# Two expert tiles in the place of filling transposes, an earlier V evacuation, and convolution taps summed in three accumulators

## The reference

```
x = x + layernorm(attn(layernorm(x)))
x = x + layernorm(ffn(layernorm(x)))

attn(x) = x + h @ Wo,   h = tele + conv + low, with q, k, v = split(x @ Wqkv), 8 heads of 16
  tele: softmax over the keys at distances 0, 1, 2, 4, ..., 512, times v at those distances
  conv: a causal convolution of v, channel by channel, with 7 taps (conv_w)
  low:  linear attention with elu(q)+1 and elu(k)+1, divided by its sum of weights
ffn(x) = sum over 8 experts of gate_e * (gelu(x @ W1[e] + b1[e]) @ W2[e] + b2[e])
         + gelu(x @ Ws1 + bs1) @ Ws2 + bs2
  gate: sigmoid(x @ gate_W) * route_scale, the two largest kept and divided by their sum
```

## Time and profile before

| | |
|---|---|
| median of 3 runs | 281.42 us (281.14 to 282.49) |
| the profiled execution, its own time | 281.83 us |
| its span, first to last instruction | 280.1 us |
| busy share of the span | PE 90%, DVE 82%, ACT 67%, POOL 30% |
| mean granted clock of PE | 0.984 of full speed |
| chain that ended last, by engine | PE 59%, ACT 20%, DVE 10%, POOL 5% |

### The profile page before, as it was taken

One profiled execution on the slowest core, in us unless ns is written; L12 is line 12 of the kernel. 1 busy time (PEld: TensorE's weight loads), 2 busy tenths in 40 slices (PEclk: granted clock), 3 DMA queues, 4 the chain that ended last, 5 costly groups with the idle time before them and its releaser, 6 DMA issues.

```text
span 280.1 us, 4721 instructions
## 1 busy us (share of the span) xinstructions
PE 252.9 (90%) x1630; PEld 176.2 (63%) x1630; DVE 228.3 (82%) x535; ACT 188.8 (67%) x445; POOL 84.5 (30%) x139
## 2 busy tenths in 40 slices
PE   5899999895978899998968899999999799999993
PEld 5444656885435686786625677777655587765483
DVE  7799999879978883999888884989689886975653
ACT  2482256538979676949789867859798356656661
POOL 5960300045471113053371213044242112330023
PEclk9999999997999999999999999999999799999998
DMA  6617801000799963401799963100799954000003
GB/s 197 150 46 241 234 28 50 1 0 9 232 233 194 223 125 67 115 1 50 211 245 194 230 126 68 37 4 20 235 220 238 227 112 83 21 2 1 1 2 112
DMA packets 23394, 32.12 MB, mean 115 GB/s; under 512 B 3957, under 2 KB 17102, under 8 KB 23370
## 3 DMA queue, kind: packets, MB, share of 16 engines
q1 hardware_dynamic: 20346, 21.59, 27.4%
q0 software_dynamic: 3024, 10.22, 19.8%
HBM read 5.07 MB, written 2.10 MB: 26 GB/s over the span
## 4 chain that ended last, share of the span: by engine, by line
PE 59%; ACT 20%; DVE 10%; POOL 5%; issue 3%; DMA 1%; POOLq 0%; DVEq 0%; ACTq 0%
PE psH L1375 11%; PE psF L1437 8%; PE psY L1477 6%; PE psG L1297 4%; PE psA L1269 4%; PE psA L1343 3%; POOL rstd L471 3%; PE psA L1477 3%; DVE prods L286 3%; ACT squares L697 3%; ACT xn L590 2%; PE psG L1463 2%; DVE prods L1026 2%; PE psH L1372 2%; PE psF L1414 2%
## 5 line engine op out<-in xcount | busy, mean ns | idle before, releaser
L286 DVE TENSOR_TENSOR prods<-qT,kT 128x1024 f32<-128x1024 f32 (+1 forms) x48 | 50.6, 1114 | 2.7 <-PE psA L1343 1.6
L469 POOL TENSOR_SCALAR var<-ss 128x4 f32<-128x4 f32 (+1 forms) x24 | 9.8, 408 | 111.9 <-ACT squares L690 49.2
L1375 PE MATMUL psH<-ident,prods 128*128 128x128 f32 x324 | 40.0, 273 | 0.0
L1375 PEld LDWEIGHTS psH<-ident,prods 128*128 128x128 f32 x324 | 36.4, 141 | 2.9 <-issue 2.9
L471 POOL TENSOR_TENSOR rstd<-var,neg_half 128x4 f32<-128x4 f32 (+2 forms) x27 | 34.8, 1288 | 2.3
L1026 DVE TENSOR_TENSOR prods<-v_shift,prob 128x896 f32<-128x896 f32 x32 | 34.5, 1078 | 0.0
L1437 PE MATMUL psF<-x3T,w 128*128 128x512 f32 x58 | 29.1, 612 | 1.8 <-ACT hid L728 1.5
L1148 DVE TENSOR_TENSOR hid<-hid,psG 128x512 f32<-128x512 f32 x30 | 19.4, 682 | 7.6 <-PE psG L1463 7.6
L728 ACT ACTIVATE hid<-psF,b1c 128x512 f32<-128x512 f32 x29 | 19.2, 683 | 7.0 <-PE psF L1437 6.9
L1343 PE MATMUL psA<-prods,slot_sel 128*32 128x512 f32 x168 | 22.6, 597 | 0.9 <-ACT fk_tok L579 0.6
L1026 DVE TENSOR_TENSOR prods<-v_tok,prob 128x128 f32<-128x128 f32 (+2 forms) x60 | 20.6, 373 | 0.6 <-DMA v_shift<-v_tok 0.5
(11 more groups left out here) (241 smaller groups left out, 579.8 us busy)
## 6 DMA issues: line engine op xcount, KB each, us to landing
v_shift<-v_tok SPq DMA_DIRECT2D x20, 448.0 KB
convT<-tapT POOLq DMA_DIRECT2D x6, 512.0 KB, 5.9
x_res<-L_attn_x SPq DMA_DIRECT2D x4, 512.0 KB, 9.8
out<-y_out SPq DMA_DIRECT2D x7, 256.0 KB, 2.3
x_in<-L_attn_x SPq DMA_DIRECT2D x3, 512.0 KB, 4.2
v_shift<-v_tok SPq DMA_DIRECT2D x4, 384.0 KB
tapT<-tapT POOLq DMA_DIRECT2D x3, 512.0 KB, 11.2
convT<-kexp POOLq DMA_DIRECT2D x3, 512.0 KB, 9.1
```

The source lines that it names most:

```text
L286: return eng.tensor_tensor(prods[:, QUADS * (s % 2) + q, t0:t1], qT[:, t0:t1], kT[:, PRE - off + t0:PRE - off + t1], ALU.mult)
L1375: ins = pe.matmul(dst, terms[:, j % TERM_BUFS, m, :], ident[:], is_transpose=True, start=False, stop=(m == live[-1]))
```

## The change

- On PE, in passes 1 to 3, `experts_out(u0, range(0, 2))` stands where the filling transposes ahead of the K projection stood (in pass 3 the second of two fillings). The tiles 2 and 3 take the places that 0 and 1 had, and the block of two tiles behind the turned logits is gone. FILL_K's own wait goes too.
- On ACT, `evacuate_v(b+1)` stands ahead of `normalise3(2b)` instead of behind it (passes 0 to 2), and in passes 1 and 2 `norm2(2b)` stands ahead of `query_parts(b+1)`.
- On POOL, the taps are summed in three accumulators. Before: 0+=1, 2+=3, 0+=4, 2+=5, 0+=6, 0+=2. Now: 0+=1, 2+=3, 4+=5, 0+=2, 4+=6, 0+=4. There are six transfers of the same size in both.
- In the last pass the turning of the gates of the last unit moves ahead of its last hidden chunk on PE and ACT, one expert tile of unit 6 moves behind the spread gates, and DVE takes the small gate steps in other portions between the large products.

```
-N_SUMS, N_SIDE = 4, 2
+N_SUMS, N_SIDE, N_LATE = 3, 1, 2
-LAST_GATE_STEPS = (5, 7, 9, N_GATE_STEPS)
+LAST_GATE_STEPS = (6, 9, N_GATE_STEPS, N_GATE_STEPS)
...
             def sum_taps_second(b):
                 pool.wait_ge(tap_scaled, upto(b - 1, TAPS, 6))
+                add_tap(b, 4, 5, late_added)
+
+            def sum_taps_third(b):
                 pool.wait_ge(sums_added, N_DMA * upto(b - 1, N_SUMS, 1))
+                pool.wait_ge(side_added, N_DMA * upto(b - 1, N_SIDE, 1))
+                add_tap(b, 0, 2, sums_added)
+                pool.wait_ge(tap_scaled, upto(b - 1, TAPS, 7))
+                pool.wait_ge(late_added, N_DMA * upto(b - 1, N_LATE, 1))
+                add_tap(b, 4, 6, late_added)
+                pool.wait_ge(sums_added, N_DMA * upto(b - 1, N_SUMS, 2))
+                pool.wait_ge(late_added, N_DMA * upto(b - 1, N_LATE, 2))
                 add_tap(b, 0, 4, sums_added)
-                pool.wait_ge(side_added, N_DMA * upto(b - 1, N_SIDE, 1))
-                add_tap(b, 2, 5, side_added)
-
-            def sum_taps_third(b):
-                pool.wait_ge(tap_scaled, upto(b - 1, TAPS, 7))
-                pool.wait_ge(sums_added, N_DMA * upto(b - 1, N_SUMS, 2))
-                add_tap(b, 0, 6, sums_added)
-                pool.wait_ge(sums_added, N_DMA * upto(b - 1, N_SUMS, 3))
-                pool.wait_ge(side_added, N_DMA * upto(b - 1, N_SIDE, 2))
-                add_tap(b, 0, 2, sums_added)
...
                         key_parts(b + 1)
+                        if ffn:
+                            norm2(2 * b)
                         query_parts(b + 1)
-                        norm2(2 * b)
+                        if b == 0:
+                            norm2(2 * b)
                         norm3_squares(2 * b)
                         norm2(2 * b + 1)
+                        evacuate_v(b + 1)
                         normalise3(2 * b)
-                        evacuate_v(b + 1)
...
-                    if more and ffn:
-                        pe.wait_ge(hidden_free, upto(u1, N_HIDDEN, -1))
-                        keep_busy(FILL_K, front(u1, X3))
+                    if ffn:
+                        experts_out(u0, range(0, 2))
                     if more:
                         project_k(b + 1)
-                    else:
-                        keep_busy(FILL_LAST, psA[:, 0, :])
                     if ffn:
                         turn_x3(u1)
-                        experts_out(u0, (0,))
+                        experts_out(u0, (2,))
                         gate_logits(u1)
-                        experts_out(u0, (1,))
+                        experts_out(u0, (3,))
                         turn_logits(u1)
-                        experts_out(u0, range(2, TPH))
...
-                    hidden(u1, range(2, 4))
+                    hidden(u1, (2,))
+                    gates_expert_major(u1)
+                    hidden(u1, (3,))
                     experts_out(u0, (0,))
-                    gates_expert_major(u1)
-                    experts_out(u0, (1,))
                     spread_gates(u1, range(0, 4))
-                    experts_out(u0, range(2, TPH))
+                    experts_out(u0, range(1, TPH))
```

More of the change, by code:

```diff
@@ L246, in block_kernel @@
         tap_scaled, sums_added, side_added = sem("tap_scaled"), sem("sums_added"), sem("side_added")
+        late_added = sem("late_added")
         first_ld, first_xn = [sem(f"first_ld{h}") for h in range(2)], [sem(f"first_xn{h}") for h in range(2)]
@@ L856, in _ @@
                     shared_hidden(u0)
-                    hidden(u1, range(0, 3))
+                    hidden(u1, range(0, 1))
                     gates_expert_major(u1)
-                    hidden(u1, range(3, 4))
+                    hidden(u1, range(1, 4))
                     shared_hidden(u1)
```

## The result

| | before | after |
|---|---|---|
| median of 20 runs each | 281.14 us (280.33 to 283.76) | 278.55 us (276.14 to 281.87) |
| the profiled execution, its own time | 281.83 us | 277.38 us |
| its span | 280.1 us | 275.6 us |
| ratio after/before, 95% interval | | 0.9864 [0.9842, 0.9886] |

A forecast was written before the change was run, and what follows sets the result against it. No engine bounds the kernel throughout: PE holds 59% of the chain of waits, ACT 20%. Terms 3.9 + 0.1 + 1.0 + 2.0 = 7.0 us off 281.83 or the 281.42 median gave 274.6 us, own range 274.0 to 275.6, wide range 272.8 to 278.0.

The forecast's parts named there:

- Passes 1 and 2, the tiles: Expert tiles in the filling's place ahead of the K projection: gain of 1.96 us a pass, 3.9 us for two passes.
- norm2 ahead: norm2 before the Q operations on ACT: counted as 0, keeping the tiles' gain; without it up to about 1.5 us a pass lost.
- V early: V evacuated before the third norm on ACT: 1.0 us ahead of pass 3, 0.1 ahead of pass 2, nothing ahead of pass 1.
- Three accumulators: New order of the tap transfers: counted as 0, between -1.5 and +1 us, in pass 3 only.
- The last pass: Edits there only reorder work while PE is busy throughout: 0, at most 0.3 us either way.
- Pass 3: Second filling goes, the last tap's landing becomes the latest for the convolution's first addition: gain 2.0 us, between 0 and 2.7.
- second rival: Filling held the clock; stretches behind the moved tiles run at 1.2 GHz, 1.7 us each, 276.3 to 279.7 us; 20%.
- The wide range: 272.8 to 278.0 us, taking in the first rival (more arrives, 273.0 to 273.9, 12%) and most of the second.

The follow-up runs named there:

- E3: The kernel before with only the two expert tiles in place of the fillings of passes 1 to 3: 278.59 us, ratio 0.9893 to the kernel before.
- E5: The changed kernel plus 18 filling matmuls on PE ahead of the turned scores in passes 1 to 3: 275.06 us, ratio 0.9756 to the kernel before.
- E2: The changed kernel with the taps summed in two accumulators in the order of the kernel before: 277.41 us, ratio 0.9876 to the kernel before.
- E1: The changed kernel plus 22 filling matmuls on PE ahead of its wait for the taps of pass 3: 276.25 us, ratio 0.9806 to the kernel before.
- E13: The changed kernel with pass 3's residual taken from x_in, so its 512 KB load goes: 273.80 us, ratio 0.9712 to the kernel before.
- E14: E13 plus 18 filling matmuls on PE ahead of the turned scores: 273.99 us, ratio 0.9739 to the kernel before.
- E10: The changed kernel without the addition of tap 6, five transfers a pass, so its result lacks that tap: 273.6 us, ratio 0.97 to the kernel before.
- E15: E14 plus the last tap sum of pass 3 done on DVE instead of by a transfer: 275.44 us, ratio 0.9776 to the kernel before.

## Why the prediction was right and where it was wrong

**Passes 1 and 2, the tiles: right.** 1.96 us was the term; pass 1 gave 2.22 us, and E3 gives 2.23 us with the tiles alone. Pass 2 gave 1.56, because 0.67 us went to a half clock that E5 takes away; without it, it is 2.23.

**norm2 ahead: 0 was right, its reason was not.** I wrote that it keeps the gain and that up to 1.5 us a pass could be lost without it. E3 lost nothing there.

**V early: right in size.** 1.11 us ahead of pass 3 (1.0 predicted), nothing ahead of pass 2 (0.1 predicted). The way was a little different: not the power but the scale stretched over DVE's products, and over two of them and not one, to 2.34 us; the power then took 1.01 us and not 1.9. The Trainium skill (SBUF — State Buffer, section "SBUF: two separate sides") says that a DVE operation with two SBUF inputs and a GpSimd operation that reads SBUF exclude each other; the trace agrees, with a scale that ends 0.05 us behind the third product.

**Three accumulators: 0 was right.** E2 shows it to 0.4 us in the profile, and its ratio is not told apart from the changed kernel's.

**The last pass: 0 was right.** From the second addition of pass 3 to the end it is 36.54 us before and after, and 36.53 us in E3, which has none of the edits there.

**Pass 3: the mechanism was right, the term too large.** I let the last tap land at the distance from the first issue that it had before, 29.6 us. It landed 30.4 us behind it, and 31.2 us in E1. That is 0.7 us of the 2.0. I had seen that transfers landed in 7.8 us where one alone took 4.5, and did not ask what else was on the way; E13 shows that the residual's load alone is worth 2 us there. But that load was on its way in the kernel before too, where the fifth issue was followed by the sixth after 7.98 us and not 9.04, so why the landing came 0.7 us later is not shown.

**The step that failed: what a new wait does to the clock.** I named the landing of the last tap as the next bound and PE as ready 2.4 to 4.1 us before the old start of the addition at 234.91, which is 0.3 to 2.0 us before that landing; it was ready 2.2 us before it. I had read in the earlier trace rows that a stretch with 1.45 us of PE's work was followed by one at 1.2 GHz. I drew the conclusion only for the places of the removed filling (second rival, 20%), not for the wait that my own sum created. It cost 1.46 us in the profiled execution, 2.7 us in those of E2 and E3 (11.35 and 11.31 us between the additions, instead of 8.65). With the 0.67 us of pass 2, the 0.7 us of the landing and the 0.17 us of pass 0, this is 3.0 us. Against it the tiles and V gave 0.6 us more than their terms, 0.1 us less came ahead of pass 2, and so 2.5 us are missing from 7.0.

**Where luck came in.** The forecast's own range of 274.0 to 275.6, which had 60%, was missed by either measure. The wide range holds by the ratio because it was drawn to take in the second rival, with one or two stretches at 1.2 GHz. Two came in the profiled execution, but none behind the moved tiles, where that rival had them: the range fits by its width and not by its reason.

**What stays open.** The profiled execution took 277.38 us, the median 278.55. By the ratios E1, E5 and E13 gain 1.6, 3.0 and 4.3 us over the changed kernel, by their profiles 0.9, 2.0 and 3.8 us. The unprofiled executions may lose more at these places, but the differences are within the intervals, and no profile shows it. Nor is it shown why the clock fell in pass 2 of the changed kernel and of E3 and not in the kernel before (see the last section). Runs of equal mean clock (0.984 or 0.985) took from 276.14 to 278.92 us, so the mean clock is not all of it.

## What to carry to other kernels

When a sum makes a transfer the next bound, price PE's wait for it twice: the wait, and the half clock that can follow; 1.5 to 2.7 us behind waits of 3.1 to 3.2 us here. Before shortening a line of transfers by its order, look at the bytes that move beside it: a 512 KB load that could be left out was worth about as much (2.1 us in the line of transfers) as DVE waited for the landing (2.29 us). A filling is best put where its time is hidden up to the next bound, and has to be tried anew when that bound moves (E14).

## What the runs showed of the hardware

- **Where the clock falls.** Ahead of the scores of pass 2, PE waited 3.15 us in six of the fourteen profiles and 2.87 us in E13; behind each of these waits stands a stretch with a granted clock of 0.50 to 0.63. In the five with the filling it waited 0.90 to 1.19 us, and the clock stayed at 1.00. In between the wait does not decide: in the kernel before one of 2.63 us was not followed by a fall, but in E3 one of 2.64 us was, to 0.52 in 144.00:147.50. The rows are those of the kernel before and of E3, and the 3.50 us ahead of each held the same work of PE (0.87 and 0.86 us):

```profile
146.19 1.14 PE L1261 MATMUL psA<-ident,prods 128*128 128x128 f32 x8 [2.63 <-ACT prods L579]
```

```profile
143.97 1.86 PE L1261 MATMUL psA<-ident,prods 128*128 128x128 f32 x8 [2.64 <-ACT prods L579]
```

- **What one transfer more on the way costs.** Leaving out a 512 KB load of another queue brought the last of six tap transfers forward by 2.1 us against the first (E13), by 1.3 us in E14; leaving out one of the six brought it forward by 4.0 us (E10).
- **A slow start that the clock column does not show.** In two of fourteen profiles (E2 and E15) the first additions stood at 52.80 and 52.44 us instead of 51.2. PE's first transposes, of the changed kernel and of E2:

```profile
8.57 1.27 PE L1265 MATMUL psA<-ident,xn 128*128 128x128 f32 x8 [0.88 <-ACT xn L597]
```

```profile
8.68 1.94 PE L1265 MATMUL psA<-ident,xn 128*128 128x128 f32 x8 [1.01 <-ACT xn L597]
```

The same eight took 0.67 us longer, the two products behind them (L1283, 128x512) 2.08 us instead of 1.12, and the granted clock is given as 1.00 in both. So an execution can lose 1.3 to 1.6 us here without a sign in that column, and two profiles should be compared by intervals, not by their ends.
